# A fused state-space, expert, attention and MLP kernel: the state layer taken in four quarters of the positions

## The reference, cut to what matters

```python
# x is (B, L, M) = (4, 512, 128); S = 64 states
x_norm = layernorm(x) * gamma + beta
xz = einsum('blm,nm->bln', x_norm, W_in) + b_in
x_p, z = split(xz, 2)
x_p, z = silu(x_p), sigmoid(z)
u = einsum('blm,sm->bls', x_p, W_xp) + b_xp
a = exp(-exp(A_log))
h_t = a * h_(t-1) + u_t                      # over the 512 positions l
ys_t = h_t @ Dmat * z_t                      # (L, B, M)
y = (einsum('lbm,nm->lbn', ys, W_out) + b_out).reshape(B, L, M)
x = layernorm(x + (x + y))
...
# 64 experts, 8 of them for each of the 2048 rows, in 4 of 8 groups; two shared experts
scores = sigmoid(x @ gate_w.T)
...
x = layernorm(x + routed + shared)
# then attention with 16 heads, and a network with weights of +1 and -1
```

## Time and profile before

| | us |
|---|---|
| median of three runs | 670.66 |
| lowest and highest | 670.47 and 672.41 |
| the profiled execution, its own time | 671.52 |
| its span, from the first to the last instruction | 669.8 |
| busy in the span: PE | 587.4 (88%) |
| DVE | 480.4 (72%) |
| ACT | 395.0 (59%) |
| POOL | 371.8 (56%) |

### The profile page before, as it was taken

The page is one execution under the profiler, slowest core; times in us unless marked ns, Lnnn a source line. Parts: engine busy times, 40 slices in busy tenths (PEclk is TensorE's granted clock), DMA queues, the critical chain, the costliest instruction groups (busy, mean ns, idle before and its releaser), DMA issues.

```text
span 669.8 us, 13038 instructions
## 1 busy us (share of the span) xinstructions
PE 587.4 (88%) x3664; PEld 370.9 (55%) x3697; DVE 480.4 (72%) x1226; ACT 395.0 (59%) x896; POOL 371.8 (56%) x398
## 2 busy tenths in 40 slices
PE   3956997929999999999886999799989999888994
PEld 2245665729999999999761333233323234344552
DVE  5488734435665656778779798778878886869886
ACT  3412443405666666667657877467777778867541
POOL 6330577777777517775707787877746000235642
PEclk9985999969999999999986999899999999999998
DMA  5997971136778768887454254225203200000001
GB/s 168 362 257 286 406 275 53 52 108 198 224 223 226 211 183 222 223 223 200 131 177 111 72 154 107 46 80 151 57 30 108 72 1 3 1 0 1 17 17 31
DMA packets 98985, 91.51 MB, mean 137 GB/s; under 512 B 10694, under 2 KB 84518, under 8 KB 98726
## 3 DMA queue, kind: packets, MB, share of 16 engines
q1 hardware_dynamic: 91262, 75.24, 36.9%
q0 software_dynamic: 7680, 15.74, 8.5%
HBM read 44.87 MB, written 45.61 MB: 135 GB/s over the span
## 4 chain that ended last, share of the span: by engine, by line
PE 49%; POOL 18%; DVE 16%; issue 8%; DMA 4%; ACT 3%; another core or an unknown queue 2%; POOLq 0%; DVEq 0%; SPq 0%; ACTq 0%
PE ps L1471 11%; PE ps L1458 8%; POOL xd L520 7%; PE ps L1586 5%; PE ps L1576 5%; POOL arena L532 4%; PE ps L1481 4%; PE ps L1566 4%; PE ps L1466 4%; DVE mx L1135 3%; DVE arena L1253 2%; DVE st L844 2%; POOL rstd L469 1%; DVE xt L855 1%
## 5 line engine op out<-in xcount | busy, mean ns | idle before, releaser
L1135 DVE TENSOR_REDUCE mx<-ps 128x2 f32<-128x1024 f32 x128 | 150.8, 1218 | 29.3 <-PE ps L1566 28.7
L747 ACT ACTIVATE big<-ps 128x512 f32<-128x512 f32 x256 | 141.1, 598 | 41.6 <-PE ps L1576 31.7
L520 POOL DMA_INDIRECT xd<-xt,idx x120 | 119.9, 999 | 60.6 <-issue 35.7
L1471 PE MATMUL ps<-arena,xbT 128*128 x496 | 96.9, 319 | 0.1
L532 POOL DMA_INDIRECT big<-od,idx x72 | 71.2, 990 | 43.0 <-issue 19.0
L1057 DVE TENSOR_TENSOR hm<-sg,ps 128x176 f32<-128x176 f32 x124 | 41.8, 337 | 65.9 <-ACT sg L686 65.1
L1576 PE MATMUL ps<-arena 128*128 128x512 bf16 (+1 forms) x234 | 80.1, 388 | 7.8 <-ACT big L747 4.8
L1566 PE MATMUL ps<-arena 125*128 125x512 bf16 (+1 forms) x256 | 71.8, 394 | 9.3 <-DVE mx L1135 9.0
L1458 PE MATMUL ps<-arena,hmT 96*128 x496 | 77.5, 279 | 1.1 <-ACT hmT L682 1.1
L1471 PEld LDWEIGHTS ps<-arena,xbT 128*128 128x128 f32 x496 | 75.9, 194 | 1.1 <-issue 1.0
L676 ACT ACTIVATE big<-ps 128x256 f32<-128x256 f32 x124 | 47.5, 383 | 47.4 <-PE ps L1458 46.8
(11 more groups left out here) (218 smaller groups left out, 990.1 us busy)
## 6 DMA issues: line engine op xcount, KB each, us to landing
big<-xd SPq DMA_DIRECT2D x62, 256.0 KB
od<-big SPq DMA_DIRECT2D x62, 256.0 KB, 2.4
arena<-scr SPq DMA_DIRECT2D x96, 96.0 KB
xd<-zeros SPq DMA_DIRECT2D x1, 8192.0 KB, 31.1
xd<-zeros SPq DMA_DIRECT2D x1, 7680.0 KB, 57.9
arena<-w_gu SPq DMA_DIRECT2D x1, 5632.0 KB
scr<-places SPq DMA_DIRECT2D x8, 384.0 KB, 2.7
arena<-w_d SPq DMA_DIRECT2D x1, 2816.0 KB
```

Of the source, the lines that this page charges most:

```text
L520: pool.indirect_dma_start(out=xd[f], out_offset=bass.IndirectOffsetOnAxis(ap=idx[:, t, k:k + 1], axis=0), in_=xt[:, t], in_offset=None).th ...
L747: act.activation(ering[:, HG * (mt % 2) + h], ps[:, 4 + h % 2, :], ACT.Exp, scale=SCALE).then_inc(exp_ready, 1)
L1135: v.tensor_reduce(mx[:, k, TB * h + 2 * a:TB * h + 2 * a + 2], ps[:, 2 * a:2 * a + 2, :], AX_X, ALU.max).then_inc(s1_free, 1)
L1471: ins = pe.matmul(ps[:, 2 + (u - GU) % 2, I2 * a:I2 * a + I2], xbT[:, (u - GU) % 2, a], wgu_s[:, bass.ds(expert(2 * (u - GU) + a), 1), :]. ...
```

## The change

- **The quarters.** The state layer is cut by positions, not by batches. Quarter c is the positions 128c to 128c+127 of all four batches (`tiles_of`, `each_of`); the loads of `x` are cut in the same way. Each quarter has its Silu, its `u`, its scan (which starts from the last state of the quarter before) and its gating. `states(c)`, `gated(c)`, `to_xp`, `to_z`, `to_u`, `to_y` and `to_out` do for one quarter what the stages did for all.
- **The order.** Quarters 0 and 1 go through to `add_mixer` and the logits of half 0 first. Quarters 2 and 3 have their states made beside that; their gating lies in `route(0)` where DVE waits for PE, their `add_mixer` behind the addresses of half 0, and their `normalise` behind the weights of the first tile.
- **POOL.** The two `rstd_of` of half 1 stand in the indirect DMAs of half 0, ahead of the third and the fourth; the memset of `arena` stands behind the `rstd_of` of half 0.
- **ACT** loads its tables four times ahead of the scores, not twice, and issues the eleven small loads of the state layer.
- **SP.** `clear_rows(0)` is issued ahead of `w_gu` and `w_d`, and `w_d` is loaded in two parts, 80 rows and 8.
- **Banks.** The quarters use banks 4 to 7, the logits of half 0 bank 0 and those of half 1 bank 5.

```diff
@@ block.sync
-            for q in range(B):
-                sp.dma_start(xt[:, TB * q:TB * q + TB, :], x.rearrange(tiled, p=P)[:, TB * q:TB * q + TB, :]).then_inc(s_x[q], 16)
+            for c in range(TB):
+                sp.dma_start(xt[:].rearrange("p (b c) m -> p c b m", c=TB)[:, c],
+                             x.rearrange("b (c p) m -> p c b m", p=P)[:, c]).then_inc(s_x[c], 16)
...
+            sp.wait_ge(s_zeros, 1)
+            clear_rows(0)
             sp.dma_start(wgu_s, w_gu).then_inc(s_we, 16)
-            sp.dma_start(wd_s[0:I], w_d).then_inc(s_we, 16)
-            sp.wait_ge(s_zeros, 1)
+            sp.dma_start(wd_s[0:80], w_d[0:80]).then_inc(s_we, 16)
+            sp.dma_start(wd_s[80:I], w_d[80:I]).then_inc(s_we, 16)
...
-            clear_rows(0)
@@ block.gpsimd
+            rstd_of(B)
+            rstd_of(B + 1)
+            pool.wait_ge(s_rstd, B + 2)
             own(pool.memset(arena[KI:P, E * I2:E * I2 + half], 0.0))
...
-            for q in range(B, 2 * B):
-                rstd_of(q)
...
+                        if f == 0 and n in (2, 3):
+                            rstd_of(B + n)
+                            if n == 3:
+                                pool.wait_ge(s_rstd, B + 4)
+                                pool.memset(dhm[:, :, :, I:KI], 0.0).then_inc(s_pads, 1)
@@ block.scalar
+            turned(0, **first)
+            turned(1, **first)
+            silu(0)
+            turned(2, **first)
+            silu(1)
+            turned(3, **first)
+            sigmoid(0)
+            sigmoid(1)
+            silu(2)
+            silu(3)
+            sigmoid(2)
+            turned(B)
+            sigmoid(3)
+            turned(B + 1)
+            scores(0)
@@ block.vector
+            def states(c):
+
+                cols = slice(P * c, P * c + P)
+                v.wait_ge(s_u, c + 1)
+                own(v.tensor_scalar(uT[:, :, cols], ps[:, X_BANK[c], 0:2 * P].rearrange("p (j l) -> p j l", j=2), b_xp_s[:], None, ALU.add))
+                if c >= 1:
+                    v.wait_ge(s_h, c)
+                for j in range(2):
+                    ins = v.tensor_tensor_scan(hT[:, j, cols], decay[:].broadcast_to([P, P]), uT[:, j, cols],
+                                               hT[:, j, P * c - 1:P * c] if c else 0.0, ALU.mult, ALU.add)
+                ins.then_inc(s_h, 1)
...
+            normalise(tmp, xt, 2)
+            v.wait_ge(s_wx, 16 * 5)
+            v.wait_ge(s_decay, 2)
+            states(0)
+            normalise(tmp, xt, 3)
+            states(1)
+            gated(0)
+            gated(1)
             add_mixer(0)
             add_mixer(1)
             normalise(xt, tmp, B)
+            states(2)
             normalise(xt, tmp, B + 1)
-            add_mixer(2)
-            add_mixer(3)
+            states(3)
...
                 if f == 0:
-                    normalise(xt, tmp, B + 2)
-                    normalise(xt, tmp, B + 3)
+                    gated(2)
+                    gated(3)
...
                 if f == 0:
+                    add_mixer(2)
+                    add_mixer(3)
...
+                    normalise(xt, tmp, B + 2)
+                    normalise(xt, tmp, B + 3)
```

More of the change, by code:

```diff
@@ new lines, in gate_in, with silu, sigmoid, scores @@
+            def gate_in(c, dst, banks, f, part, made, done):
+                act.wait_ge(made, c + 1)
+                act.activation(dst[:, c], ps[:, banks[c], :].rearrange("p (j h l) -> p h j l", h=2, l=P), f,
+                               bias=b_in_s[:, part:part + 1]).then_inc(done, 1)
+            def silu(c):
+                gate_in(c, xpT, X_BANK, ACT.Silu, 0, s_xp, s_xps)
+            def sigmoid(c):
+                gate_in(c, zT, Z_BANK, ACT.Sigmoid, 1, s_z, s_zs)
+            def scores(f):
+                act.wait_ge(s_lg, f + 1)
+                act.activation(sc[:, NT // 2 * f:NT // 2 * (f + 1), :], ps[:, LOGITS[f], :].rearrange("p (t e) -> p t e", e=E),
+                               ACT.Sigmoid).then_inc(s_lgs, 1)
@@ new lines, in _ @@
+            first = dict(scale=gamma_s[:], bias=beta_s[:])
+            turned(0, **first)
[13 more added lines that the diff above has]
+            scores(0)
+            turned(B + 2)
+            turned(B + 3)
+            scores(1)
@@ L1354, in _, with to_xp @@
-            for b in range(B):
-                pe.wait_ge(s_xzs, B + b + 1)
-                pe.wait_ge(s_h, b // 2 + 1)
-                h = S * (b % 2)
-                pe.matmul(ps[:, 4 + b, :], dmat_s[h:h + S], hT[h:h + S, b // 2], start=True, stop=True).then_inc(s_y, 1)
-            pe.wait_ge(s_wo, 16 * 4)
-            pe.wait_ge(s_one, 1)
-            for q in range(B):
+            def to_xp(c):
+                pe.wait_ge(s_trs, c + 1)
+                if c >= 2:
+                    pe.wait_ge(s_ys, c - 1)
+                pe.matmul(ps[:, X_BANK[c], :], w_in_s[:, 0:M], xT[:, L * c:L * c + L], start=True, stop=True).then_inc(s_xp, 1)
@@ L1418, in shared_expert, with places_of @@
                 pe.wait_ge(s_sh, NT)
[L1420 to L1431 removed]
+            def places_of(f):
                 pe.wait_ge(s_const, 1)
@@ L1444, in _ @@
                 ins.then_inc(s_pos, 1)
+            places_of(0)
+            for q in range(2, B):
+                to_out(q)
+            turn(B + 2, xt)
+            turn(B + 3, xt)
+            to_logits(1)
+            dense_expert()
+            places_of(1)
             shared_expert()
```

207 lines of the change are left out of this document (116 added, 91 removed).

## The result

The changed kernel took 674.62 us in the median of 11 executions, the kernel before 672.02 of 11 on the same chip: the ratio is 1.0046, with a 95% interval of 1.0031 to 1.0061. It is slower, by 0.3 to 0.6%, where I had forecast 4.3 us less. The profiled execution has a span of 671.9 us against 669.8, which is 2.1 us longer.

A forecast was written before the change was run, and what follows sets the result against it. The prediction took the wait chain to the pair loop's start, then PE, as the bound. Of 7.3 us slack, a dense expert 3.0 us later left 4.3 us gain: median 670.66 to 666.3 us, range 662.4 to 669.8.

The forecast's parts named there:

- slack of 7.3 us: Before the pair loop DVE waits 7.3 us for rows; POOL's branch can gain no more unless the dense expert starts earlier.
- when does the routing of half 0 start: State layer, new order summed with old durations: routing of half 0 starts 6.7 us earlier than at 45.46.
- term of 1.1 us for the second `normalise`: State layer, DVE: 1.1 us for this `normalise`, behind the states of quarter 2, ending at 35.5.
- Routing of half 0 at 38.8: End of the state layer's sum: routing of half 0 starts at 38.8, where it had been 45.46.
- PE's clock in the state layer: Logits ahead of the routing of half 0: 1.1 us counted for half of them.
- Zeros by 30 us, weights hidden: DMA queues: zeros land by 30 us; dense expert's weights at 52 to 61, before PE asks at 65.7.
- Rival 3: Dense expert waits for `w_d`'s last 8 rows, landing at 71 to 73: 1 to 3 us slower, chance 0.06.
- POOL at 52.7: POOL's first indirect DMA of half 0 starts at 52.7, 19.2 us earlier, no longer waiting for zeros.
- Dense expert 3.0 us later: Dense expert, behind the logits of half 1: starts at 65.7 instead of 62.66; bounds 1.2 to 5 later.
- First copy 78.8 us behind the dense expert's start: Pair loop: nothing changes behind the dense expert's start at 65.7, so the first copy comes at 144.5, not 148.82.
- ACT's issue and tables at no cost: ACT, state layer: issuing eleven loads counted as nothing, upper bound 1.5 us; two more table loads also as none.
- number 2: Waits, issue or lower clock lengthen the path 2 to 3 us; dense expert at 68 to 70, -2 to 0, chance 0.14.

The follow-up runs named there:

- memset_late: The changed kernel with POOL's memset of `arena` moved behind the 120 indirect DMAs of both halves; 669.3 us, ratio 0.9947 to the kernel before.
- before_beside_c: The kernel before, with the memset of `arena` moved behind its first `rstd_of` of the second norm; 672.52 us, ratio 1.0008.
- memset_split: The changed kernel with the memset of `arena` cut into eight pieces of the columns; 667.24 us in one execution, the kernel before 672.5 beside it.

## Why the prediction was wrong

The mechanism (two branches, and a slack of 7.3 us in one of them) was right. One step of the sum was false, the one headed "when does the routing of half 0 start": its term of 1.1 us for the second `normalise`, which ends at 35.5 there, took 6.21 us and ended at 40.1, because POOL's memset held it.

- **Routing of half 0 at 38.8**: 45.39. I followed the new order on PE, ACT and DVE and not on POOL, where the change moves a memset of 6.92 us from 14.77 to 32.57. For the second `normalise` I took the 1.11 us of the earlier trace rows; it took 6.21. In the kernel before no long POOL instruction ran beside that `normalise`; I took this for granted without naming it. The rest of the step was good: without the hold the routing starts at 38.76 and 38.23 (memset_late and its second run).
- **PE's clock in the state layer**: I took 1.1 us for half of the logits of half 0. After 6.45 us of idle time PE ran them at the lower level, 3.51 us for all, 1.55 more, and the turn ahead of them 0.4 more. It follows from the hold, since in memset_late they take 1.96.
- **Zeros by 30 us, weights hidden**: 28.9 us, and nothing waits for weights. Rival 3 (1 to 3 us slower) gave nearly the measured time, but through a mechanism that did not occur; that its time was close is chance.
- **POOL at 52.7**: 60.27, the same 6.6 us and 1 us more; without the hold 53.61 and 53.08.
- **Dense expert 3.0 us later**: 9.7 later; without the hold 3.06 (65.72). Its parts, the two `add_mixer`, the first tile's weights and the logits at 1.2 GHz, hold.
- **The slack of 7.3 us**: right. Past 70.0 each us is a loss: 72.39 - 70.0 = 2.4, and the first copy is 2.4 later. before_beside_c shows the other side of it.
- **First copy 78.8 us behind the dense expert's start**: 78.9 in the changed kernel, but 79.6 and 81.5 in the mended ones. I had 144.5; memset_split has 145.22, memset_late 147.21. Even without the fault the first copy was forecast 1 to 3 us too early. The gain of 3.6 to 4.2 us in the mended kernel agrees with the forecast of 4.3 all the same, which is in part luck.
- **ACT's issue and tables at no cost**: the issue is over at 7.0 us, and ACT's first instruction on the loaded weights starts at 8.82, where it had been 8.49. The table load of 31.89 takes 1.28 us, the instruction ahead of it ends at 31.87, and the next one starts at 33.18, directly behind. The drain of 1.38 us, which the Trainium skill (ScalarE: Activation LUTs, section What ACT_TABLE_LOAD costs) gives for each switch, is not seen on either side of it.

Of the rivals, number 2 ("the path is longer") named waits in the state layer, but with 2 to 3 us, and left the hold of one engine by another out. The chance of 0.06 for slower was too small for a sum in which one of four lists had not been followed.

## What to carry to other kernels

When a change moves work on one engine, put every engine's list beside the others in the new order, GpSimd's too: an instruction that waits for nothing can still hold VectorE. Keep long GpSimd fills away from VectorE's SBUF to SBUF float32 `tensor_scalar` on the path, or cut them into pieces. And when two branches meet, ask first which has slack: here making the one with slack earlier at the price of the other was worth nothing, and the version that gave back half of that trade was the fastest.

## What was not expected of the hardware

- A memset of 32 x 8192 float32 on POOL (6.92 us) stretched a 128 x 128 float32 `tensor_scalar` of DVE to 5.64 us, and in before_beside_c to 6.70 us. A `normalise` of four of them lost 5.1 us to one memset, 11.7 to two in a row, and 1.1 to the same memset in eight pieces.
- A load of 32 KB from ACT's queue landed after 6.0 us beside a transfer in packets of 2 KB on SP's, and after 14.7 to 28.3 us beside one in packets of 45 KB.
- Two chips ran the same kernel in 887 us instead of 672, with engines at a standstill for up to 20 us beside indirect DMAs that took their usual 0.96 us each.
